# Attention's preparing parts of two sequences, placed behind single MoE quarters instead of in two blocks, in a MoE-attention-MoE kernel on Trainium2

## The reference

```python
def _L0_attn_ref(x, Wq, Wk, Wv, Wo, Wf):
    log_f = jax.nn.log_sigmoid(x @ Wf).transpose(0, 2, 1)
    c = jnp.cumsum(log_f, axis=-1)
    scores = jnp.einsum('bhid,bhjd->bhij', q, k) * scale
    scores = scores + c[..., :, None] - c[..., None, :]
    scores = jnp.where(causal, scores, NEG)
    attn = jax.nn.softmax(scores, axis=-1)
...
def _L0_ffn_ref(hidden_states, Wg, We, be):
    probs = jax.nn.softmax(x @ Wg, axis=-1)
    top_vals, top_idx = jax.lax.top_k(probs, TOP_K)
    gates = top_vals / jnp.sum(top_vals, axis=-1, keepdims=True)
    expert_out = jnp.einsum('th,ehd->etd', x, We) + be[:, None, :]
...
x = x + 0.5 * _L0_ffn_ref(_layernorm(x, axis=-1), L0_ffn_Wg, L0_ffn_We, L0_ffn_be)
x = x + _L0_attn_ref(_layernorm(x, axis=-1), L0_attn_Wq, L0_attn_Wk, L0_attn_Wv, L0_attn_Wo, L0_attn_Wf)
x = x + 0.5 * _L0_ffn_ref(_layernorm(x, axis=-1), L0_ffn_Wg, L0_ffn_We, L0_ffn_be)
```

## Time and profile before

| | |
|---|---|
| median of 3 runs | 470.84 us (469.02 to 476.64) |
| the profiled execution, its own time | 474.27 us |
| its span, first to last instruction | 471.5 us |
| mean granted TensorE clock | 0.963 |
| busy share: TensorE, VectorE, ScalarE, GpSimd | 88%, 78%, 59%, 51% |
| first MoE layer, attention, second MoE layer | ends at about 107 us, last output of attention at 395 us, then the end |

### The profile page before, as it was taken

How to read it: one execution, slowest core, us unless ns; L and a number is a source line. 1 busy time by engine, 2 the same in 40 slices (tenths; PEclk the granted TensorE clock), 3 DMA queues, 4 the chain that set the end, 5 groups by cost and what they waited for, 6 DMA issues and landing times.

```text
span 471.5 us, 11941 instructions
## 1 busy us (share of the span) xinstructions
PE 416.7 (88%) x3472; PEld 314.3 (67%) x3488; DVE 368.6 (78%) x1316; ACT 278.8 (59%) x758; POOL 239.8 (51%) x397
## 2 busy tenths in 40 slices
PE   1888888767799999999999999999999798888884
PEld 0666656546577777777777777778777576665662
DVE  4999999886657866776786678678667448999995
ACT  4667676451156565565657566666665567666753
POOL 8965656452145445545544554454444334665554
PEclk9999999886679999999999999999999999999999
DMA  3311000033232324233332423333430000001001
GB/s 111 94 52 23 1 0 1 0 111 115 89 110 93 120 77 141 78 114 96 102 108 74 140 81 113 94 116 100 115 102 2 6 1 1 23 25 45 22 22 45
DMA packets 31905, 32.57 MB, mean 69 GB/s; under 512 B 4808, under 2 KB 28636, under 8 KB 31866
## 3 DMA queue, kind: packets, MB, share of 16 engines
q1 hardware_dynamic: 29818, 31.58, 22.2%
q10 hardware_dynamic: 2048, 0.53, 0.6%
HBM read 16.05 MB, written 15.20 MB: 66 GB/s over the span
## 4 chain that ended last, share of the span: by engine, by line
PE 54%; DVE 24%; issue 11%; POOL 5%; ACT 4%; DVEq 1%; DMA 1%; ACTq 1%; POOLq 0%
PE bank L867 13%; PE bank L882 10%; PE bank L897 9%; DVE m_lower L288 7%; PE bank L870 5%; POOL m_pair L216 2%; PE bank L985 2%; PE bank L982 2%; DVE a_neg_max L779 2%; DVE x_all L297 2%; PE bank L990 2%; PE bank L940 2%; DVE m_best_no L376 1%; DVE m_stats L335 1%; PE bank L986 1%
## 5 line engine op out<-in xcount | busy, mean ns | idle before, releaser
L779 DVE TENSOR_REDUCE a_neg_max<-bank 128x2 f32<-128x512 f32 (+1 forms) x192 | 124.3, 685 | 66.9 <-PE bank L870 66.2
L658 POOL TENSOR_SCALAR_AFFINE_SELECT a_weights<-a_weights 128x512 f32<-128x512 f32 (+1 forms) x96 | 75.6, 787 | 111.8 <-ACT a_weights L718 111.8
L718 ACT ACTIVATE a_weights<-bank 128x512 f32<-128x512 f32 x192 | 106.7, 591 | 37.6 <-PE bank L882 19.1
L867 PE MATMUL bank<-a_k_rows,a_q_rows 104*128 104x256 f32 (+1 forms) x512 | 103.7, 324 | 4.4 <-DVE a_neg_max L779 2.2
L867 PEld LDWEIGHTS bank<-a_k_rows,a_q_rows 104*128 104x128 f32 x512 | 81.8, 203 | 23.3 <-DVE a_neg_max L779 12.3
L246 ACT ACTIVATE m_scaled<-bank,m_gates 128x128 f32<-128x128 f32 x256 | 72.3, 365 | 26.0 <-PE bank L417 26.0
L216 POOL TENSOR_TENSOR m_pair<-m_scaled 128x256 f32<-128x256 f32 x64 | 48.3, 755 | 60.3 <-ACT m_scaled L246 59.9
L882 PE MATMUL bank<-a_q_rows,a_k_rows 106*128 106x512 f32 (+1 forms) x192 | 72.8, 453 | 2.7 <-ACT a_weights L718 2.7
L288 DVE SCALAR_TENSOR_TENSOR m_lower<-bank,m_gates,m_lower 128x128 f32<-128x128 f32 x192 | 65.5, 341 | 1.2
L870 PE MATMUL bank<-a_mask,a_ident 128*128 128x256 bf16 (+1 forms) x176 | 57.8, 328 | 0.0
L897 PE MATMUL bank<-a_weights,a_v 128*32 128x128 f32 x1536 | 52.7, 279 | 0.0
(11 more groups left out here) (126 smaller groups left out, 785.4 us busy)
## 6 DMA issues: line engine op xcount, KB each, us to landing
a_k_rows<-k_stage SPq DMA_DIRECT2D x16, 416.0 KB
k_stage<-a_k_parts SPq DMA_DIRECT2D x48, 128.0 KB, 1.8
q_stage<-a_q_parts SPq DMA_DIRECT2D x48, 128.0 KB, 1.8
a_q_rows<-q_stage SPq DMA_DIRECT2D x64, 96.0 KB
x_all<-in_L_attn_x SPq DMA_DIRECT2D x8, 256.0 KB, 2.9
out_x<-x_all SPq DMA_DIRECT2D x8, 256.0 KB, 2.3
a_q_rows<-a_max_t ACTq DMA_DIRECT2D x64, 8.0 KB, 1.9
we<-in_L_ffn_We SPq DMA_DIRECT2D x1, 512.0 KB, 3.9
```

Source lines behind the costliest of these rows:

```text
L658: nc.gpsimd.affine_select(out=diagonal, in_=diagonal, compare_op=ALU.is_ge, fill=0.0, base=0, pattern=[[0, heads.stop - heads.start], [1, P]],
L718: nc.scalar.activation(weights[n // 2][:, half:half + 4, :].rearrange("p h n -> p (h n)"), wt_bank[n % 2][:, :], ACT.Exp).then_inc(wt_exp, 1)
L779: nc.vector.tensor_reduce(neg_max[:, t, first:first + heads], score_bank[p % 2][:, :].rearrange("p (h n) -> p h n", h=heads), AX.X, ALU.ma ...
L867: nc.tensor.matmul(bank[:, n * keys:(n + 1) * keys], q_rows[b][0:KR, h, t * P:(t + 1) * P], k_rows[b][0:KR, h % NU, 0:keys], start=n == 0, ...
```

## The change

Before, MoE groups 0 to 5 run alone, then the six parts of step -2 stand in group 6 and those of step -1 in group 7, three parts (3, 4, 5) at the end of each group without a quarter between them. Now MoE groups 0 to 3 run alone (the loop has one trip less, groups 2 and 3), then twelve times one attention part and one MoE quarter alternate: parts 0 to 3 of step -2 ahead of the quarters of group 4, parts 4 and 5 of step -2 and 0 and 1 of step -1 ahead of those of group 5, parts 2 to 5 of step -1 ahead of those of group 6. Group 7 runs alone after that. No instruction is added or taken away except the loop's own. SyncE's order is unchanged. The new file has three lines more above the layers, so L416 of before is L419 there.

```diff
--- before.py
+++ after.py
@@ -33,13 +33,14 @@
 
 
     lo, hi = body
-    for i in range(first, lo):
+    for i in range(first, min(lo, last)):
         step(i, i)
         if after is not None:
             after(i)
-    with eng.Fori(0, (hi - lo) // unroll) as k:
-        for part in range(unroll):
-            step(k * unroll + (lo + part), lo + part)
+    if hi > lo:
+        with eng.Fori(0, (hi - lo) // unroll) as k:
+            for part in range(unroll):
+                step(k * unroll + (lo + part), lo + part)
     for i in range(hi, last):
         step(i, i)
 
@@ -47,8 +48,8 @@
 def run_layers(eng, moe1, attention, moe2, groups, seqs, after=None):
 
 
-    def moe_steps(part, first, last, after=None):
-        run_steps(eng, lambda i, s: [part(i, s, k) for k in range(4)], first, last, (2, groups - 2), 2, after)
+    def moe_steps(part, first, last, body, after=None):
+        run_steps(eng, lambda i, s: [part(i, s, k) for k in range(4)], first, last, body, 2, after)
 
     def beside(order, i_attention, moe, i_moe):
 
@@ -59,14 +60,16 @@
             else:
                 moe(i_moe, i_moe, done)
 
-    moe_steps(moe1, -2, groups - 2, after)
-    beside("amamammaaa", -2, moe1, groups - 2)
-    beside("amamammaaa", -1, moe1, groups - 1)
+    moe_steps(moe1, -2, groups - 4, (2, groups - 4), after)
+    for at in range(12):
+        attention(-2 + at // 6, -2 + at // 6, at % 6)
+        moe1(groups - 4 + at // 4, groups - 4 + at // 4, at % 4)
+    moe_steps(moe1, groups - 1, groups, (groups, groups))
     run_steps(eng, lambda i, s: [attention(i, s, k) for k in range(6)], 0, seqs - 1, (2, 2 + (seqs - 5) // 3 * 3), 3)
     beside("amaamamaam", seqs - 1, moe2, -2)
     beside("amaamamaam", seqs, moe2, -1)
     beside("aaaamamamm", seqs + 1, moe2, 0)
-    moe_steps(moe2, 1, groups)
+    moe_steps(moe2, 1, groups, (2, groups - 2))
 
 
 def constants(nc, ctx, w, c):
```

## The result

| | median us | range, runs | mean |
|---|---|---|---|
| before | 470.84 | 468.9 to 476.64, 5 | 471.9 |
| after | 476.71 | 476.3 to 480.8, 5 | 477.6 |

The ratio is 1.0153, with a 95% interval of 1.0103 to 1.0202: the change made the kernel slower by 1 to 2%. The predicted time was 473.1 us (466 to 480); the forecast of the sign holds, and the median is 3.6 us above the predicted value. It moved by 5.9 us where 2.3 were forecast.

A forecast was written before the change was run, and what follows sets the result against it. VectorE was taken to set the pace in the first MoE layer. The third bank 1.8 us later, with 3.5 us of new waits counted, plus 0.5 for the clock gave +2.3 on 470.84: 473.1 us, range 466 to 480.

The forecast's parts named there:

- the forecast's own range: Whole kernel: -1.9 us with no new wait to +5.8 with twice the waits, 469 to 476.6 us; chance 0.42.
- rival 3: Index 4 to 7: TensorE's clock falls and stays down, 8.4 us on top of the 2.3, 481.5 us; chance 0.13.
- The bound (VectorE) and the conserved work: First MoE layer: VectorE sets the pace; 9.02 us of attention parts stay, 47.20 us of work from index 4's start.
- The chain over a_f: Seam of index 4 and 5: query and key wait for ScalarE's a_f, TensorE idle from 71.5 to 73.5 us.
- The new waits at full clock: VectorE at biases of index 5, 6, 7 and index 6's third quarter: 3.5 us in place of 2.20 + 0.52.
- The clock: Index 4 to 7: at least three TensorE pauses of 1.2 to 2.1 us, priced together at 0.5 us.
- What is won behind MoE's end: Scores start some 0.15 us after MoE's end without DMA wait; third bank at 114.6 instead of 112.78, +1.8 us.
- The signs that I had set down: VectorE waits 1 to 2 us, TensorE over 1.5 for a_f, scores within 0.3 of MoE's end, MoE ends 110 to 113.
- Rivals 1 and 4: 1: new waits hide, gaps fill, -3.0, 467.8 us, chance 0.16. 4: losses and gains balance, 470.8 us, chance 0.12.
- rival 2: First sequence's attention step runs at full clock, 15.41 us falls to 11.0, 4.4 won, 468.7 us; chance 0.17.

The follow-up runs named there:

- e1: Changed kernel with ScalarE's copy a_f one part earlier (part 3) in steps -2 and -1; mean 473.6 us, ratio to before 1.0040.
- e8: Changed kernel with only step -2 in the new place, step -1 in index 7 as before; mean 474.4 us, ratio to before 1.0112.
- e2: Changed kernel with ten idle matmuls ahead of waits of parts 2 to 4 (step -2), 2 and 4 (step -1); mean 472.8 us, ratio to before 1.0058.
- the second profile: Changed kernel run again unchanged, on the same chip; mean 477.8 us, ratio to before 1.0131.
- e3: Changed kernel with the twelve parts one group later, behind quarters of index 5, 6 and 7; mean 474.8 us, ratio to before 1.0089.
- e9: Kernel before with parts spread within index 6 and 7, copy a_f a part earlier and one wait more; mean 471.1 us, ratio 0.9944.
- e10: Kernel before with parts spread within index 6 and 7, early copy a_f, and ten idle matmuls ahead of the parts' waits; mean 470.0 us, ratio 1.0032.
- e11: Kernel before with the early copy a_f alone; mean 471.2 us, ratio 1.0004.
- e4: Changed kernel with both the early copy a_f and the idle matmuls ahead of the parts' waits; mean 472.6 us, ratio to before 1.0118.
- e6: Kernel before with the parts spread between the last quarters within index 6 and 7; mean 471.1 us, ratio 1.0101.
- e5: Changed kernel with early copy a_f and the twelve parts one group later; mean 472.1 us, ratio to before 1.0019.
- e7: Kernel before with 16 idle matmuls ahead of the first scores; mean 472.3 us, ratio 1.0070.

## Why the prediction was right, and where it was off

**How near it was.** The sign is right, the size is not: 5.9 us by the medians instead of 2.3. The median of 476.71 lies just above the forecast's own range (469 to 476.6, at most twice the waits) and inside the stated one, which was widened for half of rival 3. That it ended inside is owed to that width and to a gain behind MoE that was greater than I had it (below).

**The bound (VectorE) and the conserved work.** Right. VectorE's busy time is the same (367.9 and 368.6 us), and none of the 9.02 us was removed. The 47.20 us of work and 8.4 of waits make 55.6; MoE took 55.68.

**The chain over a_f.** Right, to 0.15 us. From index 4's start, I had a_xt copied at 8.1 us and Wf starts at 8.06 (71.11); I had a_f at 12.5 and query starts at 12.64 (75.69), idle 1.94 where I had 2.0. e1 removes that chain and wins 4.2 us; e8 leaves half of it and half of the loss.

**The new waits at full clock.** Right. 1.7, 0.5, 0.8 and 0.5 were forecast. Three of them can be read with the clock held by e2, 1.28, 1.00 and 0.80; the bias of index 6 is best read in the changed kernel, where the clock was 1.00 from 80 to 96 us, 0.71. That is 3.8 us instead of 3.5. Its gate copy stands behind a_v and a_xt on ScalarE, as forecast.

**The clock: the step that failed in size.** I wrote "I add 0.5 us for them". In the changed kernel the waits sum to 2.87 + 0.71 + 2.49 + 1.24 + 0.26 + 0.80 = 8.4 us, 4.9 over the 3.5, and the two greatest are 3.1 us above what they are with the clock at 1.00 (e2). Such a pause can cost more than itself here, because the tile behind it then runs at 1.2 GHz, and that tile is already late. The pause of 1.46 us before gave me the pattern (half clock, then a wait of 1.12), and I should have priced some of the new ones with it: two at 1.2 us would have given 475. Which ones can't be told from their length: the waits of 1.82 and 1.37 us before 67.90 and 71.11 left the clock at 1.00, and in the second profile the same 1.82 did not.

The Trainium skill, "TensorE: Matmul & The Clock Gate", section "Why this matters for your kernels", says that idle gaps between bursts bring back the half rate; its row speaks of longer gaps than the two that count here. The traces agree with it in part: 0.58 behind the pause of 1.94 us and 0.50 within three us of the one of 1.52, but 1.00 behind the same pause of 1.94 in e3.

**What is won behind MoE's end.** Right, and more than forecast. Scores start 0.22 us after MoE's end (I had 0.15), the block of step -1's parts is gone and the row DMA hidden. The first two banks took 1.64 us (118.95 to 120.59) where I had 2.74 at half clock. So the third bank came 5.75 us later: the 1.8 of the forecast and 5.0 for MoE, less 1.1 for these banks. It could not pay for MoE's 9.3 us.

**The signs that I had set down.** Two of the signs of being right did not come: VectorE waited 2.87 and 2.49 us where I had 1 to 2, and MoE ended 55.7 us after the start of index 4, not 49 to 52 (110 to 113 us). The waits for a_f, and the scores' start without a DMA wait, did come. The time from the third bank to the end is 358.5 us and was 358.8 before, so the loss of this pair of profiles lies ahead of that bank: 5.75 us at the seam and 2.06 before index 4, which is scatter. One figure of the prediction does not come out of its own terms: without new waits and without the clock's 0.5 the sum is -1.7, where I wrote -1.9.

**The rivals.** Rival 3, the slower one, was half true. The mechanism and place are those, but the clock did not stay down: 0.90 over 60 to 110 us, with falls of some 3, 3 and 7 us. Rivals 1 and 4 did not occur. A first sequence at full clock, rival 2's case, does occur, but in e2, e9, e10 and e11 and not because of the change, and it takes 13.3 to 13.5 us from fifth bank to fifth bank.

**What stays open.** How the loss divides between the chain and the clock: e1 gives back 4.2 us at the same mean clock, e2 5.0 with the chain left in, and together they give no more. e1 is still 2.7 us above the kernel before by the means, and by the ratio not clearly so. The two measures of the smaller differences do not agree (e4, e6, e9, e10). And the profiles of the changed kernel hold a second cost that I did not foresee, told below.

## What to carry to other kernels

When work is spread between tiles on in-order engines, follow every handshake of a moved part through all engines: a part that needs a copy from an engine must have that copy ahead of the quarter in between, not behind it. Price a pause on TensorE with the slow tile that may follow it: in these traces the same pause of 1.8 or 1.9 us was followed by half clock in one execution and not in another, and where it was, the wait behind it was about twice as long (2.87 and 2.49 us instead of 1.28 and 1.00). And if the whole gain is bounded by a few us of idle time, the new waits need only a few us to turn the sign.

## What the runs showed of the hardware that was not expected

**The first sequence's step has three lengths.** The distance from the fifth bank of row maxima of sequence one to that of sequence two was 18.6 to 18.9 us in six profiles with a mean granted clock of 0.59, 15.4 in four at 0.83, and 13.3 to 13.5 in four at 0.97 or 0.98, in unlike kernels and without a pattern (14 profiles, two of them of the changed kernel). The same stretch in the changed kernel's two profiles and in e9:

```profile
124.86:143.50 18.64, 16.15 (x63) 12.08 (x63) 11.13 (x24) 4.82 (x13) 4.14 (x6) 0.59 0.25 77
```

```profile
124.10:139.50 15.40, 12.50 (x64) 9.65 (x63) 10.92 (x24) 4.79 (x13) 4.14 (x6) 0.83 0.28 86
```

```profile
114.48:127.76 13.28, 10.38 (x64) 7.81 (x63) 10.88 (x25) 4.34 (x12) 3.83 (x6) 0.98 0.38 118
```

The 5.4 us between them are as much as the change itself, and they are a likely part of the 10 us scatter of every kernel here. In the two profiles that the prediction compares, before and after, the step was 18.77 and 18.64, so it is not in their difference.

**The second MoE layer has three lengths too.** From the fifth bank of the last sequence to the end it is 107.8 to 108.6 us in five profiles whose clock over the first 30 us of this stretch is 1.00, 109.1 to 110.0 in four at 0.94, and 111.7 to 112.8 in five at 0.83, again in unlike kernels. The changed kernel's two profiles are at 107.8 and 111.7, the one before is at 110.0. The 30 us in the changed kernel, before, and in the changed kernel's second profile:

```profile
371.28:401.28 30.00, 27.13 (x310) 19.90 (x309) 17.38 (x73) 20.06 (x50) 13.08 (x24) 1.00 0.01 2
```

```profile
361.55:391.55 30.00, 26.53 (x292) 18.91 (x291) 16.06 (x64) 18.92 (x46) 11.16 (x20) 0.94 0.01 3
```

```profile
367.26:397.26 30.00, 27.41 (x285) 19.87 (x283) 15.08 (x57) 17.87 (x42) 10.54 (x19) 0.83 0.01 2
```

**A slower step in the attention loop.** From the fifth bank of the fourth sequence to that of the fifth it takes 16.4 us in the profile before, but 18.2 and 17.7 in the two of the changed kernel, and 17.3, 17.4, 17.7 and 17.3 in e1, e3, e5 and e8, at a clock of 1.00 throughout; 16.4 in e2, e4, e6, e7, e9, e10 and e11. In the changed kernel ScalarE issues two DMAs there and is held longer by them, and its next exponential comes late. SyncE issues two DMAs at the same time, and they are longer too:

```profile
189.27 2.12 ACTq L713 DMA_DIRECT2D a_q_rows<-a_max_t  x2
...
191.50 1.08 ACT L721 ACTIVATE a_weights<-bank 128x512 f32<-128x512 f32 x2 [1.66 <-PE bank L885]
```

```profile
189.51 1.99 SPq L609 DMA_DIRECT2D k_stage<-a_c_parts  x2
```

Before, at the same place:

```profile
180.45 1.17 ACTq L710 DMA_DIRECT2D a_q_rows<-a_max_t  x2
...
181.73 0.60 ACT L718 ACTIVATE a_weights<-bank 128x512 f32<-128x512 f32 x1 [0.71 <-issue]
```

```profile
177.72 2.65 SPq L602 DMA_DIRECT2D q_stage<-a_q_parts  x3
180.70 1.01 SPq L606 DMA_DIRECT2D k_stage<-a_c_parts  x2
```

The issue of the same two DMAs takes 2.12 us instead of 1.17. It lies in the loop's first trip, in just those kernels whose six parts of step -2 begin in index 4 or 5 without the idle matmuls. In all six of their profiles the long issue of ScalarE (1.5 to 1.9 us for one DMA) starts 0.05 us before one of SyncE that is as long. Before, one of SyncE's issues is as long (1.67 of the 2.65 us), but it comes at 178.2 us, when ScalarE issues nothing. In e4, e7 and e9 such a pair comes later, at 344, 345 and 304 us, and there the step is 0.7 to 0.8 us longer than in the other kernels. So a step can grow where an issue of ScalarE is long, and in these profiles that one is long together with one of SyncE. What makes them long, and why the change shifts it here, is open, and no run was made on it. The 1.3 and 1.8 us of the changed kernel's two profiles would be a part of its loss if other executions have them too. In the pair that the prediction compares they are balanced by the second MoE layer, which was 2.2 us shorter.
